# A macaron transformer block with relative attention on one core: one pool of six PSUM banks, and relative scores laid out head by head

## The reference

```python
x = x + 0.5 * ffn(layernorm(x), Wg, Wu, Wd)      # 8 experts of 512, all summed
x = x + attention(layernorm(x), w_q, w_k, w_v, w_o, rel_emb)
x = x + 0.5 * ffn(layernorm(x), Wg, Wu, Wd)
# ffn: acc += (silu(x @ wg) * (x @ wu)) @ wd, for each expert
# attention, 16 heads of 8, rotary q and k, causal:
scores = q @ k.T + einsum("bhqd,qkd->bhqk", q, rel)   # rel = rel_emb[clip(k - q, -32, 32) + 32]
attn = softmax(scores)
ctx = attn @ v + einsum("bhqk,qkd->bhqd", attn, rel)
out = ctx @ w_o.T
```

## Time and profile before

| | us |
|---|---|
| median of 3 runs | 1520.03 (1515.97 to 1520.62) |
| the profiled execution | 1518.37 |
| its span, first to last instruction | 1516.6 |
| PE busy | 1403.2 |
| DVE busy | 1319.6 |
| ACT busy | 1123.6 |
| POOL busy | 1087.7 |

### The profile page before, as it was taken

How to read it: one execution, slowest core, us unless ns; L and a number is a source line. 1 busy time by engine, 2 the same in 40 slices (tenths; PEclk the granted TensorE clock), 3 DMA queues, 4 the chain that set the end, 5 groups by cost and what they waited for, 6 DMA issues and landing times.

```text
span 1516.6 us, 28935 instructions
## 1 busy us (share of the span) xinstructions
PE 1403.2 (93%) x8632; PEld 1076.7 (71%) x8632; DVE 1319.6 (87%) x2541; ACT 1123.6 (74%) x2642; POOL 1087.7 (72%) x956
## 2 busy tenths in 40 slices
PE   8999999899999999899899899989999998999898
PEld 6777667677676767677677667767777776677686
DVE  5888898999899989999899888999999988899665
ACT  6656868788687877787777687777887876778654
POOL 7867777687678766877668677686777875767655
PEclk9999999999999999999999999999999999999999
DMA  5405999999999999999999999999999999998200
GB/s 178 132 29 153 170 206 180 170 198 172 167 200 181 167 171 186 172 177 176 162 187 187 165 172 171 169 187 166 181 181 171 206 167 173 154 172 146 55 0 8
DMA packets 716380, 241.42 MB, mean 159 GB/s; under 512 B 650304, under 2 KB 679744, under 8 KB 716224
## 3 DMA queue, kind: packets, MB, share of 16 engines
q1 hardware_dynamic: 716224, 239.57, 86.6%
HBM read 77.34 MB, written 69.86 MB: 97 GB/s over the span
## 4 chain that ended last, share of the span: by engine, by line
PE 28%; DVE 14%; SPq 9%; DMA 8%; issue 5%; ACT 4%; POOL 1%; ACTq 0%; POOLq 0%; DVEq 0%
PE hidden L697 5%; PE hidden L698 5%; PE hidden L699 5%; SPq L667 4%; DMA probs_t<-probs 3%; DVE work L1108 3%; DVE negmax L1113 3%; DVE hid L1017 3%; PE acc L771 3%; DVE hid L1011 2%; PE acc L774 2%; PE acc L772 2%; DMA band_t<-bands 2%; PE work L822 2%; SPq L655 1%
## 5 line engine op out<-in xcount | busy, mean ns | idle before, releaser
L1163 POOL TENSOR_TENSOR hid_lo<-hid,hid_hi 128x512 fp32r<-128x512 f32 x512 | 661.7, 1296 | 276.3 <-ACT hid_hi L897 272.3
L892 ACT ACTIVATE hid<-hidden 128x512 f32<-128x512 f32 x512 | 306.9, 603 | 155.3 <-PE hidden L699 144.0
L1011 DVE SCALAR_TENSOR_TENSOR hid<-hid,hidden 128x512 f32<-128x512 f32 x512 | 347.7, 680 | 75.3 <-ACT hid L892 73.8
L897 ACT CAST hid_hi<-hid 128x512 fp32r<-128x512 f32 x512 | 320.1, 626 | 105.6 <-DVE hid L1017 62.4
L1017 DVE TENSOR_TENSOR hid<-hid,hidden 128x512 f32<-128x512 f32 x512 | 348.3, 681 | 17.9 <-PE hidden L699 10.7
L697 PE MATMUL hidden<-xt,wu 128*128 128x512 f32 x512 | 218.0, 426 | 25.0 <-DVE hid L1011 23.7
L1178 POOL TENSOR_TENSOR probs<-lent_p,probs 128x512 f16<-128x512 f32 (+1 forms) x160 | 171.9, 1074 | 91.6 <-ACT probs L954 91.2
L1108 DVE TENSOR_TENSOR work<-work,rel_win 128x160 f32<-128x160 f32 (+2 forms) x352 | 192.1, 551 | 40.9 <-PE work L822 38.9
L697 PE MATMUL hidden<-xt,wg 128*128 128x512 f32 x512 | 212.8, 416 | 15.0 <-DVE hid L1017 11.2
L1113 DVE TENSOR_REDUCE negmax<-work 128x1 f32<-128x384 f32 (+3 forms) x352 | 222.6, 636 | 2.3
L771 PE MATMUL acc<-hid_hi,wd 128*128 128x512 f32 x512 | 211.7, 413 | 0.1
(11 more groups left out here) (100 smaller groups left out, 2235.7 us busy)
## 6 DMA issues: line engine op xcount, KB each, us to landing
rel_win<-rel_window_scratch SPq DMA_DIRECT2D x128, 320.0 KB, 3.5
prob_window_scratch<-probs SPq DMA_DIRECT2D x384, 80.0 KB, 2.2
q_scratch<-rope SPq DMA_DIRECT2D x16, 512.0 KB, 4.1
qq<-q_scratch SPq DMA_DIRECT2D x32, 256.0 KB
rel_window_scratch<-g_s SPq DMA_DIRECT2D x32, 256.0 KB, 3.9
k_scratch<-rope SPq DMA_DIRECT2D x16, 512.0 KB, 4.6
kk<-k_scratch SPq DMA_DIRECT2D x32, 256.0 KB
prob_window_scratch<-probs SPq DMA_DIRECT2D x32, 256.0 KB, 3.3
```

Of the source, the lines that this page charges most:

```text
L892: act.activation(hid[:, arg % HB, :], hidden[2 * arg % 3][:, :], ACT.Tanh, scale=0.5).then_inc(s_tanh, 1)
L897: act.copy(hid_hi[:, arg % 2, :], hid[:, arg % HB, :]).then_inc(s_hhi, 1)
L1011: dve.scalar_tensor_tensor(out=hid[:, arg % HB, :], in0=hid[:, arg % HB, :], scalar=1.0, in1=hidden[2 * arg % 3][:, :], op0=ALU.add, op1=A ...
L1163: pool.tensor_tensor(hid_lo[:, arg % 2, :], hid[:, arg % HB, :], hid_hi[:, arg % 2, :].bitcast(F32), ALU.subtract).then_inc(s_hlo, 1)
```

## The change

Three things change, and some with them:

- **Banks.** The three banks of `hidden` go into the pool: `BANKS` is 6, and gate and up take banks through `take_bank` like the others. Gate's bank is given back by gated, up's by product. In the plan gate n follows gated n-2 (before: product n-2) and up n follows product n-2 (before: gated n-1).
- **Layout.** Relative scores lie head by head: `g_s`, `rel_win` and the scratch have each head's values side by side. A row of the scratch holds 16 strips of 160 places, one for each head and tile of a group; the store writes strips of 32 places where it wrote runs of 128.
- **Plan.** A gate, up, down or project that starts later than PE's clock, or after a task of one of the first two tiles, is charged 0.1 us more; the costs of qk_store, band_turn, recip_wide, exp, p_lent and store_band are other numbers.
- Lent exponentials have two buffers (`exps`, `EB`), so exp of a lent task waits for the lent task two before. The copies "hi" and of a lent "p_hi" are multiplications by 1.0. The array of maxima holds two groups.

```diff
+    EB = 2
...
+    lents_to = [sum(lent(x) for x in range(k)) for k in range(B * NK)]
+    lent_tasks = [k for k in range(B * NK) if lent(k)]
+
+    def lent_before(k, by):
+
+        return lent_tasks[lents_to[k] - by] if lents_to[k] >= by else None
...
-        step("PE", 0.695, at, "gate", n, ("product", back(n, 2)), split[0], *normed)
+        step("PE", 0.695, at, "gate", n, ("gated", back(n, 2)), split[0], *normed)
...
-        step("PE", 0.695, at + 1, "up", n, ("gated", back(n, 1)), split[1], *normed)
+        step("PE", 0.695, at + 1, "up", n, ("product", back(n, 2)), split[1], *normed)
...
-            step("SP", 0.6, at, "qk_store", (t, i), ("qk_lo", (t, i)),
+            step("SP", 1.3, at, "qk_store", (t, i), ("qk_lo", (t, i)),
...
-            step("SP", 1.8, at, "band_turn", gg, ("load_band", NT * gg + NT - 1), ("band_values", back(gg, 1)), lands=LATE)
+            step("SP", 1.4, at, "band_turn", gg, ("load_band", NT * gg + NT - 1), ("band_values", back(gg, 1)), lands=LATE)
...
-            step("POOL", 1.25, at - 7, "recip_wide", gg, ("recip", gg), ("outproj", back(gg, 1)))
+            step("POOL", 1.0, at - 7, "recip_wide", gg, ("recip", gg), ("outproj", back(gg, 1)))
...
-            step("ACT", HEADS[i] * 0.16 + 0.12 + columns / 1200, due[k] + 1, "exp", k, ("largest", k),
-                 ("p_lent", k - 2 if lent(k) and lent(k - 2) and k >= 2 else k - 3 if lent(k) and k >= 3 else None))
+            step("ACT", HEADS[i] * 0.235 + columns / 1200, due[k] + 1, "exp", k, ("largest", k),
+                 ("p_lent", lent_before(k, EB) if lent(k) else None))
...
-                step("POOL", 0.05 + columns / 425, due[k] + 2, "p_lent", k, ("p_hi", k))
+                step("POOL", 0.04 + columns / 475, due[k] + 2, "p_lent", k, ("p_hi", k))
...
-            step("SP", 1.1 if HEADS[i] == 2 else 0.55, due[k] + 2.5, "store_band", k, lower(k),
+            step("SP", 1.2 if HEADS[i] == 2 else 0.62, due[k] + 2.5, "store_band", k, lower(k),
...
-    BANKS = 3
-    TAKES = {"scores": ("bank", "done_with"), "qrel": ("bank", "qrel_copy"), "recip_turned": ("bank", "recip_copy"),
+    BANKS = 6
+    TAKES = {"gate": ("bank", "gated"), "up": ("bank", "product"), "scores": ("bank", "done_with"), "qrel": ("bank", "qrel_copy"), "recip_turned": ("bank", "recip_copy"),
...
+        if name in ("gate", "up", "down", "project") and (start > clock["PE"] or after_short):
+
+            takes += 0.1
+        if engine == "PE":
+            after_short = name == "scores" and TASKS[arg % NK][1] < 2
...
-        rel_win = sb("rel_win", [P, WB, W, HQ])
+        rel_win = sb("rel_win", [P, WB, HQ, W])
...
-        lent_p = sb("lent_p", [P, L])
+        exps = sb("exps", [P, EB, L])
...
-                    sp.dma_start(bass.AP(zwin_t, arg % 2 * NT * HQ * TILE + HQ,
-                                         [[HQ * (W + 1), P], [HQ * TILE, NT], [1, R * HQ]]), g_s[:, :, :]
-                                 ).then_inc(s_gst, 16)
+
+                    sp.dma_start(bass.AP(zwin_t, arg % 2 * NQ * TILE + 1, [[NQ * W + 1, P], [W, NQ], [1, R]]),
+                                 g_s[:, :, :].rearrange("p i (a r) -> p (i a) r", r=R)).then_inc(s_gst, 16)
...
-                    sp.dma_start(rel_win[:, arg % WB, :, :].rearrange("p c a -> p (c a)"),
-                                 bass.AP(zwin_t, (gg % 2 * NT + i) * HQ * TILE, [[HQ * W, P], [1, HQ * W]])
+                    sp.dma_start(rel_win[:, arg % WB, :, :].rearrange("p a c -> p (a c)"),
+                                 bass.AP(zwin_t, gg % 2 * NQ * TILE + i * HQ * W, [[NQ * W, P], [1, HQ * W]])
                                  ).then_inc(s_win[arg % WB], 16)
...
+                    if was == "gate":
+                        pe.wait_ge(s_act, x + 1)
+                    if was == "up":
+                        pe.wait_ge(s_hid, x + 1)
...
-                    wait(pe, s_hid, arg - 1)
-                    three(hidden[2 * arg % 3][:, :], wg[:, HI, e, cols], wg[:, LO, e, cols],
+                    bank = take_bank(name, arg)
+                    three(bank[:, :], wg[:, HI, e, cols], wg[:, LO, e, cols],
                           x_hi, x_lo).then_inc(s_gate, 1)
...
-                    wait(pe, s_act, arg)
-                    three(hidden[(2 * arg + 1) % 3][:, :], wu[:, HI, e, cols], wu[:, LO, e, cols],
+                    bank = take_bank(name, arg)
+                    three(bank[:, :], wu[:, HI, e, cols], wu[:, LO, e, cols],
                           x_hi, x_lo).then_inc(s_up, 1)
...
-                    act.copy(hid_hi[:, arg % 2, :], hid[:, arg % HB, :]).then_inc(s_hhi, 1)
+                    act.mul(hid_hi[:, arg % 2, :], hid[:, arg % HB, :], 1.0).then_inc(s_hhi, 1)
...
-                        wait(act, s_plent, lents[arg] - 1)
+                        wait(act, s_plent, lents[arg] - EB)
...
-                        act.copy(probs[:, arg % PB, 0:cols], lent_p[:, 0:cols]).then_inc(s_phi, 1)
+                        act.mul(probs[:, arg % PB, 0:cols], exp_of(arg)[:, 0:cols], 1.0).then_inc(s_phi, 1)
...
-                    dve.tensor_tensor(near, near, rel_win[:, quad % WB, lo:W, places[0]:places[-1] + 1].rearrange(
-                        "p c a -> p a c"), ALU.add).then_inc(s_near, 1)
+                    dve.tensor_tensor(near, near, rel_win[:, quad % WB, places[0]:places[-1] + 1, lo:W],
+                                      ALU.add).then_inc(s_near, 1)
...
-    rel_g, rel_g0 = np.zeros((HQ, 4, DH, R, HQ), rel.dtype), np.zeros((HQ, 4, DH, R, HQ), rel.dtype)
+    rel_g, rel_g0 = np.zeros((HQ, 4, DH, HQ, R), rel.dtype), np.zeros((HQ, 4, DH, HQ, R), rel.dtype)
```

More of the change, by code:

```diff
@@ L401, in macaron_kernel @@
         raw_c = raw_rel[:, 2 * P:3 * P].rearrange("p (a s d) -> p a s d", a=HQ, d=DH)
-        window = rel_win[:, 2, :, :].rearrange("p c a -> p (c a)")
-        hidden = [pb(f"hidden{i}", [P, L]) for i in range(3)]
+        window = rel_win[:, 2, :, :].rearrange("p a c -> p (a c)")
         acc = pb("acc", [P, L])
@@ L519, in exp_of @@
         def exp_of(k):
-            return lent_p if lent(k) else work[bank_of["scores", k]]
+            return exps[:, lents_to[k] % EB, :] if lent(k) else work[bank_of["scores", k]]
         def turned_probs(k):
@@ L710, in take_bank @@
                     was, x = held
+                    if was == "gate":
+                        pe.wait_ge(s_act, x + 1)
+                    if was == "up":
+                        pe.wait_ge(s_hid, x + 1)
+                    if was == "scores" and not lent(x):
+                        pe.wait_ge(*lower_part(x))
                     if was == "scores" and lent(x):
@@ L713, in take_bank @@
                         pe.wait_ge(s_exp, unit(quad, places[-1]) + 1)
-                    elif was == "scores":
-                        pe.wait_ge(*lower_part(x))
                     if was == "qrel":
@@ L734, in _ @@
             for i in range(24):
-                done = pe.transpose(hidden[0][:, 0:P], ident[:, :], ident[:, :])
+                done = pe.transpose(work[0][:, 0:P], ident[:, :], ident[:, :])
             done.then_inc(s_warm, 1)
@@ L738, in _ @@
             pe.wait_ge(s_xn, 1)
-            transposes(hidden[2], xn).then_inc(s_xnt, 1)
+            transposes(work[2], xn).then_inc(s_xnt, 1)
             for name, arg in order:
@@ L884, in _ @@
             act.wait_ge(s_xnt, 1)
-            act.copy(xt[0][:, HI, :], hidden[2][:, :]).then_inc(s_xhi, 1)
+            act.copy(xt[0][:, HI, :], work[2][:, :]).then_inc(s_xhi, 1)
             split_expert(0, 2)
@@ L891, in _ @@
                     wait(act, s_hlo, arg + 1 - HB)
-                    act.activation(hid[:, arg % HB, :], hidden[2 * arg % 3][:, :], ACT.Tanh,
+                    act.activation(hid[:, arg % HB, :], work[bank_of["gate", arg]][:, :], ACT.Tanh,
                                    scale=0.5).then_inc(s_tanh, 1)
@@ L953, in _ @@
                     if lent(arg):
-                        act.copy(probs[:, arg % PB, 0:cols], lent_p[:, 0:cols]).then_inc(s_phi, 1)
+                        act.mul(probs[:, arg % PB, 0:cols], exp_of(arg)[:, 0:cols], 1.0).then_inc(s_phi, 1)
                     else:
-                        act.mul(probs[:, arg % PB, 0:cols], work[bank_of["scores", arg]][:, 0:cols],
-                                SCALE).then_inc(s_phi, 1)
+                        act.mul(probs[:, arg % PB, 0:cols], exp_of(arg)[:, 0:cols], SCALE).then_inc(s_phi, 1)
                 if name == "recip_copy":
@@ L1004, in _ @@
             norm_shift(0)
-            norm_lo(0, xt[0], hidden[2])
+            norm_lo(0, xt[0], work[2])
             split_down(0)
@@ L1011, in _ @@
                     dve.scalar_tensor_tensor(out=hid[:, arg % HB, :], in0=hid[:, arg % HB, :], scalar=1.0,
-                                             in1=hidden[2 * arg % 3][:, :], op0=ALU.add,
+                                             in1=work[bank_of["gate", arg]][:, :], op0=ALU.add,
                                              op1=ALU.mult).then_inc(s_act, 1)
```

(5 more changed lines are left out.)

24 lines of the change are left out of this document (11 added, 13 removed).

## The result

| | before | after |
|---|---|---|
| median, us | 1519.16 (1515.97 to 1520.62) | 1554.74 (1546.34 to 1559.07) |
| ratio, 95% interval | | 1.023 (1.018 to 1.028) |
| the profiled execution, us | 1518.37 | 1546.34 |
| its span, us | 1516.6 | 1544.5 |

The kernel became 2.3% slower, about 35 us. The prediction said 1464 us and faster; the time lies beyond the upper end of its range (1522), where its fourth rival stood.

A forecast was written before the change was run, and what follows sets the result against it. It took PE and DVE, running close together in a written order, as the bound, with PE waiting 92.9 us for gated and product. 1518.4 - 67 + 11 = 1462.4, the median 1.7 above: 1464 us, range 1427 to 1522.

The forecast's parts named there:

- fourth rival: Store of relative scores: small pieces cost a full write each, turned probabilities land late; up to 1554 us, chance 0.05.
- 0 in the sum: Store of relative scores: its 45 us on the DMA engines are hidden, so it adds 0 us.
- upper bound of 2.8: Store of relative scores: 1536 more packets at the mean price, 2.8 us per DMA engine, 90 over 32 stores.
- D: Small pieces in the store: 90 us on the DMA engines, late turned probabilities, up to 1554 us; chance 0.05.
- 67 us for banks and DVE's room: Middle stretch: gate and up wait less, and DVE's 1082 us at its old share allow 1193 us, 67 less.
- rival A: Waits move on to down, values and bands while DVE keeps its price; -31 + 11, 1500 us, chance 0.20.
- The share of 0.907: DVE's busy share of the 1260 us middle stretch, taken to stay the same after the change.
- +11 for waits on banks: Shared pool: 1551 bank takes at today's rate give 7 us of PE waits, half as much again makes +11.
- the 20 us that were named: Profile sign: no wait of scores, qrel or gate on banks over 20 us in all.
- rival B: Shared banks block PE when attention and feed-forward hold all six; 1538 us, chance 0.11.
- The plan's costs at 0: Written order under the new plan costs: between -33 and +33 us, taken as 0.

The follow-up runs named there:

- e17: The changed kernel in its own order and contiguous reading, but with the old store, fill and load (scores go to wrong places): 1494.1 us, 0.986.
- e7: The kernel before with the layout alone, its 2048 pieces of 128 bytes aligned by leaving out the shift from row to row: 1532.5 us, 1.012.
- e1: The kernel before with the head-by-head layout alone, old banks and old order: 1587.4 us, 1.045.
- e9: The kernel before with contiguous reading of the old window, store and load still interleaved (scores go to wrong places): 1509.1 us, 0.997.
- e5: The changed kernel with the old layout and old plan costs, so six shared banks with second exponentials buffer and multiplications by one: 1500.0 us, 0.990.
- e6: The kernel before with scratch rows of sixteen strips, heads still interleaved, 512 pieces of 512 bytes: 1513.0 us, 1.000.
- e4: The kernel before planned with the new cost numbers and the 0.1 us charge: 1535.1 us, 1.009.
- e3: The changed kernel planned with the cost numbers of before and no 0.1 us charge: 1544.0 us, 1.016.
- e14: The six-banks kernel (old layout, old costs) planned with turned probabilities landing after 6.5 us: 1503.5 us, 0.990.
- e16: The six-banks kernel (old layout, old costs) with a third buffer for "hi" and one lent exponentials buffer: 1501.0 us, 0.989.
- e8: The changed kernel with the store of relative scores issued from ScalarE's queue: 1564.7 us, 1.033.
- e11: The kernel before with the layout alone, storing 8 of 16 strips (1024 unaligned pieces of 128 bytes): 1527.5 us, 1.009.

## Why the prediction was wrong

**The step that failed first: "0 in the sum" for the store.** The prediction priced it at 1.4 us on the DMA engines for each store, 45 in all, and held that to be hidden, because the queue of loads waits for its landing only 5 times and windows are needed late. Measured in packet time it is 4.5 us on each engine for each store (after against e17), above even its upper bound of 2.8; on the landing it is 3.1 (7.0 against 3.9), and at the end of the kernel 1.8: 3.7%, some 56 us. Two things were wrong in the reasoning. The price was the mean of all packets, halved by the look of band DMAs, whose stores in 320-byte pieces land after 2.2 us and whose loads in 1024 pieces after 3.1; those rows say nothing of 2048 pieces of 128 bytes, at starts that move by 4 bytes from row to row. And the cover was looked for only among those who wait for this store. That cover held: the loads' queue waits for this store's landing 9.6 us in after, 3.9 before. Those who pay are others, issued within 7 us behind it: the transposes (5.74 us to landing against 4.23 for the rest) and the loads of bands (5.87 against 3.50). On their landing PE stands in its written order.

**The rival that came true** was the fourth, D: turned probabilities land late and the time goes up to 1554. Its sign in the profile, PE's wait for turned probabilities over 60 us, is there with 81.5. That its time fits to the microsecond is luck: 1464 + 90 contains a gain of 56 us, of which some 22 came (e17), and a price of 90, of which some 56 arrived. Its chance of 0.05 was small for a part that adds to a DMA share of 0.99, though 0.99 is no ceiling: in after stretches reach 1.45. Its reason was half right. The Trainium skill ("DMA: Bandwidth & Descriptors", Specifications) says that below 512 bytes a transfer is read, modified and written; by size alone e7 should then cost what e1 costs. It costs 1.2% over before instead of 4.5, so size alone doesn't set the price. Nor do the places alone: the old store's 512-byte pieces start 16 bytes further against a multiple of 128 from row to row, and are cheap. What was dear in these runs is small pieces whose starts move by 4 bytes a row. Pieces of 512 bytes that move by 4, or of 128 that move by 16, weren't run, so whether the old store is cheap for its size or for its step isn't shown.

**The second step: 67 us for banks and DVE's room.** The banks alone gave 1.0% (15 us), the contiguous reading alone 0.3% (5), both 1.5% (22). So even without the store the forecast of 1464 would have missed by about 30: after's order without the dear store is 1494 (e17), near rival A's 1500. The share of 0.907 that DVE was held to keep is not a pace: with 47 us less work DVE was simply idle for longer (1108.3 of the same 1260 us in e9, 0.880). And the waits of gate and up were counted as time of PE, though where PE waits less for one thing it arrives earlier at the next: "hi" on "down" 37.5 to 64.2, values 32.6 to 40.7 in e5. That the waits move on was rival A's mechanism, if not for its reason, since DVE did get cheaper.

**The third: +11 for waits on banks.** PEld's waits of takers on other tenants' banks, without gate and up on gated and product, add up to some 34 us in after (turns 9.8, scores 9.4, gate and up 10.1, qrel 4.5) against some 8 before. The size was off by more than a factor of two; each kind stays below the 20 us that were named, and the blocked bank of rival B did not come.

**What held.** The additions (314, 483 and 687 expected, 327, 495 and 695 measured), DVE's total (near 1260; 1262.2), gate's and up's waits (under 30; 24.2, though with the banks alone they are 51.8, so the other parts had a share in it), "hi" as a multiplication (9 ns more; what that does to the time wasn't run by itself), and long rows as such (e6). The store was to land 1 to 2 us later "with no new wait of DVE on it": DVE's new wait on a window is 3.7 us, but it landed 3.1 later, and that was the point. The plan's costs at 0 were inside their bounds, on the bad side: e4 and e3 say 0.7 to 0.9%, of the size by which orders of the same work differ anyway.

**What stays open.** Where the remaining 1.5% of e7 over e9 comes from (its store lands 0.8 us later than e9's 4.0 and takes only 8 us more packet time on each engine). What made 13 of the 24 stands late one by one. What sets the pace of about 1500 us once the store is out: with the banks shared, taking away the values' wait (e14) or that of "hi" (e16) gains nothing. Whether the shift can be had without small unaligned pieces wasn't tried. Why the store on ScalarE's queue (e8) is dearer still is open. Of the kernels with the whole computation the best measured is e5, at 1500.0 us.

## What to carry to other kernels

Price a DMA not only by who waits for it but by what is issued behind it and who stands in order for that; a store cut into small pieces that start off a multiple of their size is worth a run by itself before it buys anything on an engine. Busy time saved on an engine can be worth next to nothing (47 us of DVE gave 5), and of waits that add up to 93 us a change may remove 41 and give back 15. With a planned order, time other orders of the same work too: here they lay 0.8% below to 0.9% above the kernel before.

## What the runs showed of the hardware

- 2048 pieces of 128 bytes written to DRAM land after 7.0 to 8.3 us where their starts move by 4 bytes against a multiple of 128 from row to row, and after 4.8 at multiples of 128; 512 pieces of 512 bytes, whose starts move by 16 bytes, after 2.8 to 4.1. The unaligned ones took 120 (e1 against e9) to 144 us (after against e17) more packet time on each DMA engine over 32 stores, the aligned ones 8.
- In after the last packet of such a store ends 3.45 us after the end of the issuing instruction (medians over the 32 stores), and the store counts as landed at 6.66; in before it is 1.99 and 3.44. From the last packet to the landing it is 3.15 us in after, 0.67 in before and 0.81 with aligned pieces (e7): most of what the store lost lies behind its last packet.
- Half as many unaligned pieces (e11) took 14 us more packet time on each engine than e9, all of them 120.
- After a stand of 5 us PE went on at its lower clock level for part of the next 4 us (granted clock 0.60). In after the granted clock is below 0.75 for 87 us in all, in e17 for 59, in before for 29, in e1 for 121.
